# Two residual convolution blocks on one core: smaller column additions, later waits, other PSUM pairs, fewer filler matmuls

## The reference

```python
x = x + conv1x1(attention(dwconv3x3(conv1x1(layernorm(groupnorm(x))))))   # 8 heads, 2 key/value heads, softmax over channels
g = groupnorm(x)
x = x + conv1x1(concat(conv1x1(g, w1), conv3x3(g, w3), conv5x5(g, w5), conv3x3_dilated2(g, wd)), wf)
```

## Time and profile before

| | us |
|---|---|
| time, median of 3 runs (1895.88 to 1897.46) | 1895.9 |
| the profiled execution's own time | 1904.7 |
| its span, first to last instruction | 1902.9 |
| TensorE matmul busy | 1791.7 (94%) |
| VectorE busy | 1474.5 (77%) |
| ScalarE busy | 1032.9 (54%) |
| GpSimd busy | 537.1 (28%) |

### The profile page before, as it was taken

The page is one execution under the profiler, slowest core; times in us unless marked ns, Lnnn a source line. Parts: engine busy times, 40 slices in busy tenths (PEclk is TensorE's granted clock), DMA queues, the critical chain, the costliest instruction groups (busy, mean ns, idle before and its releaser), DMA issues.

```text
span 1902.9 us, 42762 instructions
## 1 busy us (share of the span) xinstructions
PE 1791.7 (94%) x14516; PEld 1711.8 (90%) x14516; DVE 1474.5 (77%) x1886; ACT 1032.9 (54%) x1736; POOL 537.1 (28%) x315
## 2 busy tenths in 40 slices
PE   4999998999999999899999999989999999989998
PEld 3899978999999997899989998989998999789998
DVE  4777568999786647999968655899987765689997
ACT  0756466555285646554536764745536564665551
POOL 5599800322281000123237000022325400003222
PEclk9999989999999998999999999889999999899999
DMA  7012103666501200556630210256661120035553
GB/s 186 0 39 74 34 16 92 159 167 159 141 4 58 72 2 15 130 156 166 169 87 13 67 53 1 48 145 169 159 158 43 37 71 25 1 92 135 132 134 95
DMA packets 101476, 166.83 MB, mean 88 GB/s; under 512 B 40040, under 2 KB 74568, under 8 KB 101224
## 3 DMA queue, kind: packets, MB, share of 16 engines
q1 hardware_dynamic: 79624, 138.63, 29.1%
q10 hardware_dynamic: 21760, 27.03, 4.4%
HBM read 52.86 MB, written 25.17 MB: 41 GB/s over the span
## 4 chain that ended last, share of the span: by engine, by line
PE 70%; DVE 12%; issue 9%; POOL 2%; ACT 2%; SPq 2%; DMA 2%; DVEq 1%; ACTq 0%; POOLq 0%
PE ps L762 25%; PE ps L646 11%; PE ps L661 7%; PE ps L663 7%; PE ps L662 7%; PE ps L672 6%; PE ps L700 4%; PE ps L620 2%; DVE region L1327 2%; DVE region L1310 2%; DVE region L1219 2%; DVE region L1279 1%; DMA X<-in_x_dram 1%; POOL region L539 1%; DVE region L1230 1%
## 5 line engine op out<-in xcount | busy, mean ns | idle before, releaser
L762 PE MATMUL ps<-region,W 128*96 128x256 f16 (+3 forms) x7316 | 820.8, 272 | 41.4 <-DVE region L1327 18.2
L762 PEld LDWEIGHTS ps<-region,W 128*96 128x96 f16 (+1 forms) x7316 | 798.5, 123 | 61.1 <-DVE region L1327 22.3
L927 ACT ACTIVATE region<-region 96x1056 f16<-96x1056 f32 (+3 forms) x168 | 208.2, 1284 | 296.0 <-DVE region L1226 283.1
L1141 DVE TENSOR_TENSOR region<-V,band 128x2322 f32<-128x2322 f32 x96 | 261.9, 2731 | 125.0 <-PE ps L663 124.1
L549 POOL TENSOR_TENSOR region<-region,X 96x1536 f32<-96x1536 f32 (+1 forms) x44 | 124.1, 2820 | 589.7 <-DVE region L1343 589.7
L559 POOL TENSOR_TENSOR region<-region 96x1056 f32<-96x1056 f32 (+1 forms) x36 | 85.1, 2365 | 684.1 <-ACT region L908 682.8
L1310 DVE SCALAR_TENSOR_TENSOR region<-ps,small,region 96x768 f32<-96x768 f32 (+1 forms) x220 | 204.2, 989 | 50.9 <-ACT region L980 38.3
L661 PE MATMUL ps<-region 128*128 x1152 | 224.1, 276 | 7.3 <-POOL region L539 6.7
L663 PE MATMUL ps<-region 128*128 x1152 | 222.7, 275 | 0.0
L662 PE MATMUL ps<-region 128*128 x1152 | 222.2, 274 | 0.0
L646 PE MATMUL ps<-proj,region 96*128 96x240 f32 x1024 | 214.9, 374 | 0.0
(11 more groups left out here) (167 smaller groups left out, 2043.0 us busy)
## 6 DMA issues: line engine op xcount, KB each, us to landing
region<-region SPq DMA_DIRECT2D x108, 247.5 KB, 3.8
region<-in_x_dram SPq DMA_DIRECT2D x128, 192.0 KB, 2.4
out_dram<-region SPq DMA_DIRECT2D x40, 576.0 KB, 4.2
region<-region ACTq DMA_DIRECT2D x80, 247.5 KB, 2.4
X<-in_x_dram SPq DMA_DIRECT2D x30, 576.0 KB, 6.0
region<-region SPq DMA_DIRECT2D x36, 247.4 KB, 4.9
X<-in_x_dram SPq DMA_DIRECT2D x19, 384.0 KB, 14.9
region<-region SPq DMA_DIRECT2D x24, 185.6 KB, 3.2
```

The costliest lines, as they stand in the source:

```text
L762: last = mm(o, w, src, start=k == 0, stop=k == len(steps) - 1, skip_group_check=split and ck > 0)
L927: act.activation(dst[0:C, a:e, x:z], src, ACT.Copy).then_inc(s_h, 1)
L1141: v.tensor_tensor(T[:, i].rearrange("p m (i j) -> p m i j", j=3), taps.broadcast_to([P, DM, BW // 3, 3]), mask.broadcast_to([P, DM, BW // ...
```

## The change

1. Even units use bank pairs (0, 4, 2, 6, 0), and both kinds of unit await the previous unit's last rows at g = 2.
2. At g = 0 of every unit (before: only of the first) the low-part matmuls of kinds 1 and 2 are put behind the high parts of kind 0, and the wait for the low parts' transfers stands there.
3. `outputs` makes four additions (row 1 of both columns, then rows 0 and 2 of both) instead of two. `first_point` awaits only the first two of them; `first_rows` now awaits all four.
4. `differences` of GpSimd is awaited before `points_1`, not before `wide`; `point_0_and_inf` comes first, after a wait for `wide`.
5. Three transfers of `place_first(b, 1)` are issued on ScalarE.
6. 8 instead of 22 fillers before the mean of the second norm; at the start of an image TensorE awaits the last rows, not the outputs.

```diff
-    BANKS = ((0, 2, 4, 6, 0), (2, 4, 0, 6, 2))
+    BANKS = ((0, 4, 2, 6, 0), (2, 4, 0, 6, 2))
...
-                place_first(b, 1)
+                place_first(sync, b, 1, groups=False)
...
-                pe.wait_ge(s_acc, b * UNITS * NACC + START)
+                pe.wait_ge(s_acc, (b * UNITS - 1) * NACC + 7 + START)
                 keep_warm(0, 2)
...
-                keep_warm(0, 22)
+                keep_warm(0, 8)
...
-                        elif g == 1 + i:
+                        elif g == 2:
                             pe.wait_ge(s_acc, (n - 1) * NACC + 7 + START)
...
-                        split, late = first and g in (0, 2), []
+                        split, late = g == 0 or first and g == 2, []
...
                             if split and ck == 0:
-                                pe.wait_ge(s_firstlo[g // 2], (b + 1) * FIRSTLO + START)
+                                if first:
+                                    pe.wait_ge(s_firstlo[g // 2], (b + 1) * FIRSTLO + START)
+                                else:
+                                    pe.wait_ge(s_extlo[i], (b * 5 + k2 + i) * EXTLO + START)
...
-                                if g == 0 and c == 0 and k == n_high and not first:
-                                    pe.wait_ge(s_extlo[i], (b * 5 + k2 + i) * EXTLO + START)
...
-                    act.wait_ge(s_acc, n * NACC + START)
+                    act.wait_ge(s_acc, (n - 1) * NACC + 9 + START)
...
                 highs(0, 0, 0, lambda: rows_normed(1, 1))
+                place_first(act, b, 1, tiles=False)
...
-                    if whole > 1:
-                        dve.wait_ge(s_eta, b * (UNITS - 2) + u - 1 + START)
+                    if whole == UNITS - 1:
+                        dve.wait_ge(s_zero, b + 1 + START)
...
-                        points_1()
-                        done(2)
-                        point_0_and_inf()
+                        if whole > 1:
+                            done(2)
+                            point_0_and_inf()
+                            dve.wait_ge(s_eta, b * (UNITS - 2) + u - 1 + START)
+                            points_1()
+                        else:
+                            points_1()
+                            done(2)
+                            point_0_and_inf()
...
                     dve.wait_ge(s_cv, n * NCV + 2 + START)
+                    dve.wait_ge(s_acc, n * NACC + START)
                     step(2, 1, OSC_MSIXTH, 1)
...
-                    for c in range(2):
-                        v.tensor_tensor(grid[:, c], kind(1 + c), kind(0), ALU.add).then_inc(s_acc, 1)
+                    for rows in (slice(1, 2), slice(0, 3, 2)):
+                        for c in range(2):
+                            v.tensor_tensor(grid[:, c, rows], kind(rows, 1 + c), kind(rows, 0), ALU.add).then_inc(s_acc, 1)
```

More of the change, by code:

```diff
@@ L97, in sb @@
             return ctx.enter_context(nc.sbuf_tensor(name, shape, dt))
-        START = 4
+        START = 8
         counted = []
@@ L287, in build_program @@
         s_out = sem("output_written")
-        NPL, NH, NL, NCV, NACC = 8, 8, 4, 5, 9
+        NPL, NH, NL, NCV, NACC = 8, 8, 4, 5, 11
         s_wt = plain_sem("weights_placed")
@@ L319, in value, with place_groups, place_first @@
                 return self.base + self.n
+        def place_groups(queue, signal, dst, low, at, m, k, part):
+            x, z, end = PARTS[part]
+            last = z - x
+            queue.dma_start(dst[64:96, :, x:z - 2], low[64:96, :, x + 2:z]).then_inc(signal, 16)
+            queue.dma_start(lo[64:96, at:at + m, z:end], low[64:96, k:k + m, z:end]).then_inc(signal, 16)
+            queue.dma_start(lo[96:P, at:at + m, z:end - 1], low[64:96, k:k + m, z + 1:end]).then_inc(signal, 16)
+        def place_first(queue, b, part, tiles=True, groups=True):
+            low = buffers(0)[1]
+            x, end = PARTS[part][0], PARTS[part][2]
+            signal = s_firstp[part]
+            queue.wait_ge(s_l, b * UNITS * NL + 2 * part + 2 + START)
+            if tiles:
+                queue.dma_start(hi[C:P, 0:5, x:end], low[0:32, :, x:end]).then_inc(signal, 16)
+                queue.dma_start(hi2[C:P, 0:5, x:end], low[32:64, :, x:end]).then_inc(signal, 16)
+                queue.dma_start(lo[0:32, 0:5, x:end], low[64:96, :, x:end]).then_inc(s_firstlo[part], 16)
+                queue.dma_start(lo[32:64, 0:5, x:end - 1], low[64:96, :, x + 1:end]).then_inc(s_firstlo[part], 16)
+            if groups:
+                place_groups(queue, s_firstlo[part], lo[:, 0:5], low, 0, BPU, 1, part)
         @block.sync
@@ L369, in place_weights @@
                 assert len(places) == NPLACES
[L371 to L389, removed]
             def place_low(b, u):
@@ L402, in place_low @@
                 for part in range(2):
-                    place_groups(s_extlo[i], lo[:, a:e], low, 5 * i, nb, 0, part)
+                    place_groups(sync, s_extlo[i], lo[:, a:e], low, 5 * i, nb, 0, part)
             def write_out(b, u):
@@ L421, in _ @@
                     place_weights()
-                place_first(b, 0)
-                place_first(b, 1)
+                place_first(sync, b, 0)
+                place_first(sync, b, 1, groups=False)
                 place_low(b, 1)
@@ L1338, in outputs @@
                     grid = ob.rearrange("p (k i j c) -> p c i k j", i=OR, j=HC, c=2)[:, :, :, 0:blocks]
-                    kind = lambda c: acc[:, :, c, 0:blocks * HC].rearrange("p i (k j) -> p i k j", j=HC)
+                    kind = lambda rows, c: acc[:, rows, c, 0:blocks * HC].rearrange("p i (k j) -> p i k j", j=HC)
                     dve.wait_ge(s_acc, n * NACC + 7 + START)
                     dve.wait_ge(s_out, n * 16 + START)
-                    for c in range(2):
-                        v.tensor_tensor(grid[:, c], kind(1 + c), kind(0), ALU.add).then_inc(s_acc, 1)
+                    for rows in (slice(1, 2), slice(0, 3, 2)):
+                        for c in range(2):
+                            v.tensor_tensor(grid[:, c, rows], kind(rows, 1 + c), kind(rows, 0), ALU.add).then_inc(s_acc, 1)
                 def window(m, i, k2, whole):
```

## The result

The changed kernel takes 1883.3 us (median of 4 runs, 1881.2 to 1884.9) against 1895.9: ratio 0.9931, 95% interval 0.9914 to 0.9948. It is faster, by 12.6 us; the forecast said 39.4 and 1856.5, and its range (1834 to 1877) doesn't hold the time. The profiled execution took 1882.0 with a span of 1880.3; that of before took 1904.7. Between the two profiled executions lie 22.6, and these can be laid out by stretch.

What follows compares the result with a forecast made beforehand. It took a loop of VectorE and ScalarE (19.59 a window) as the bound, TensorE's own work at 18.84 a unit. 18.8 + 7.9 + 12.8 - 0.1 = 39.4 off 1895.9 gave 1856.5; range 1834 to 1877.

Steps and rivals of the forecast that it cites:

- Window, the four additions, the later wait, the port: Middle window of VectorE: period 19.51 against 19.58, 0.07 gained, with `wide` held by GpSimd's SBUF port until the differences end.
- The later wait for the differences brings nothing in a middle window: Middle window: by the port rule, awaiting GpSimd's differences after `wide` instead of before it gains nothing.
- Fillers: Second norm's mean: sixteen fillers instead of 44 instructions end before VectorE can use the mean; 7.9 gained over the run.
- Phase of TensorE, 18.8: Units: TensorE, no longer pinned late by pauses at g = 1, gains 4.7 per image, 18.8 for four.
- Units 9 and 10 are TensorE's own work, so the start of unit 9 carries through to the end of the image: Last two units: an earlier start of unit 9 is kept to the image's end; lag gain 2.73 per image.
- priced the place where it was read at 0.35: Four of the run's nine waits for the mean, 0.35 each, left out of the 7.9 gained there.
- Between images, 3 x (1.57 + 0.5): Three changes of image: TensorE restarts behind the last rows, 1.57 earlier, plus 0.5 in each pair of fillers.
- Idle is now 0.9: Change of image: TensorE's idle falls from 2.46 to 0.9, less than the 1.39 that never lowered the clock.
- Between images, 6.6 for the clock: Line 646 in images 2 to 4: the clock stays high, gaining 2.5 + 2.5 + 1.6 = 6.6.
- The median is 8.8 below the profiled run; I take that as kept: Final sum: the gain was subtracted from the median 1895.9, not the profiled 1904.7, giving 1856.5 instead of 1865.3.
- the clock's 8.1: Between images, rival: the clock still falls, 8.1 less gained, time 1864.6; chance 10%.

Runs made afterwards that it cites:

- half_residual: Changed kernel with GpSimd adding X to only the left half of each residual's elements (output incomplete): 1856.3 us, ratio 0.9790.
- eta_first: Changed kernel with GpSimd's differences awaited before `wide` again, the later steps' order kept: 1891.3 us, ratio 0.9971.
- two_additions: Changed kernel with the outputs in two additions as before, both awaited by ScalarE: 1893.1 us, ratio 0.9977.
- late_residual: Changed kernel with GpSimd's residual of unit 9 started only once the next image's spread is handed to TensorE: 1876.2 us, ratio 0.9896.
- store_scalar: Changed kernel with unit 8's store issued on ScalarE's queue after its residual, its next-image rows loaded with unit 9's: 1883.2 us, ratio 0.9928.
- pe_unrolled: Changed kernel with TensorE's program written out four times instead of looping over the images: 1875.2 us, ratio 0.9884.
- before_again: The kernel before the change, unedited, run once more for a second profile: 1897.8 us, ratio 0.9996.
- after_again: The changed kernel, unedited, run once more for a second profile: 1884.0 us, ratio 0.9935.

## Why the prediction was wrong, by its steps

- **Window, the four additions, the later wait, the port:** right to 0.04 in the mean period (19.51 against 19.55, to 0.01 in every other window) and shown from both sides (half_residual, eta_first, two_additions). "The later wait for the differences brings nothing in a middle window" was too strong: it brings 0.24 (eta_first). The page "SBUF — State Buffer" of the Trainium skill, section "Who interferes with whom", is borne out, for an instruction of 96 elements as well (2.90 against 0.15). The rule of the page "VectorE: DVE Perf Modes" of the Trainium skill, section "The TRN2 errata", would have given outputs of 2.13, an estimate with its 0.157 for each addition more (1.82 + 2 x 0.157); they take 1.96.
- **Fillers:** right as far as the runs can tell (8.0, uncertain by 3 to 4, against 7.9).
- **Phase of TensorE, 18.8:** the size was right, and the step "Units 9 and 10 are TensorE's own work, so the start of unit 9 carries through to the end of the image" failed. Unit 9 starts earlier as forecast, but between the points of unit 10 stands a chain through VectorE that TensorE had been too late to feel. It now waits 1.6 to 2.2 for line 1078, and loses 1.4 to 1.6 at half clock twice. These are 10.9 of the 13.4 missed; the other 2.5 are not traced. The chain is late by two delays: line 1077 shares the SBUF port with the residual (2.90), and the outputs ahead of it await a store (1.0 to 1.7). late_residual takes the first away alone, store_scalar the second; the wait falls to nothing in the one and to 0.47 at most in the other, and the stretch gives 18.9 and 13.0. The hold stood in the earlier trace rows with its 2.46, in unit 10 itself and with 0.06 between its chain and TensorE's next step; the prediction used it for `wide` only and priced the place where it was read at 0.35.
- **Between images, 3 x (1.57 + 0.5):** the restart was worked out from the wait that the profile names; behind it stood the outer loop's branch, up to 3.7 long in before, which had run under the wait for the outputs and left 0.4 of room. "Idle is now 0.9" became 1.92; pe_unrolled has 0.91. By the profiles 3.7 were missed here.
- **Between images, 6.6 for the clock:** the number was right against the first profile (51.86 in every image), by luck twice over. Over half of it was that execution's own: at the changes of image the first profile of before lost 8.5, the second 3.4. And the clock stayed up although the pause was 1.92 and not the 0.9 that the forecast rested on.
- **"The median is 8.8 below the profiled run; I take that as kept":** wrong, and the second largest piece, 10.1. No such distance is kept: the profiled execution lies 1.3 above the median in before_again, 1.3 below in the changed kernel and 3.3 below in after_again. Terms read from an execution that lies 8.8 above the median can't all be owed to the median as well: the clock term was counted in full, and the 8.8 that it partly made up was then taken off again. By the second profile of before, with one such place (line 646 at 54.34, and its fillers) instead of three, the clock's 8.1 would have been 3.0, and the forecast 5.1 nearer.

## What to carry to other kernels

When an engine is moved earlier, list everything that it awaits between its old and its new place, to the end of the loop, however small; a wait that was covered by the old lag has no row of its own before. Place each row that you read in its stage: the row that told of the port stood in the very chain that became the limit. Where a row shows an engine held by a neighbour, look for the same pair elsewhere, for a 96x1 instruction on a critical chain beside a large one of GpSimd above all, and delay the large one. Read losses that come and go (half clock) from two executions, and take a sum made on one execution against that one's own repeat, not against the median with the difference kept.

## What the runs showed of the hardware

- The back edge of TensorE's outer loop (a branch in its queue) takes 3.4 to 3.6 us at the median in both kernels, and 4.8, at most 5.9, in store_scalar, where one more load of rows is issued some 5 us before it; whether that load lengthens it is not shown. Straight code for four images has no such pause. What the branch spends the time on is not shown either.
- VectorE subtracts 96 numbers in 0.15, or in 2.90 if a GpSimd instruction that reads SBUF was issued 0.02 before it; it ends with that instruction or within 0.03 of its end.
- Pauses of about 2 us of TensorE are followed by half clock in some images and not in others of the same execution (9.74 and 8.11 for the same 93 matmuls), each time for about 1.7 or 3.4 us lost in all. At the changes of image it came behind 15 of 30 pauses of 1.8 to 2.8, and behind none of 9 pauses of 0.91 or less.
